# A graph network on one core: first part rearranged, with idle-time products, widened products and held-back loads

## The chip, the cores and the metric

The kernel runs on one core of one Trainium2 chip. The metric is the time of one execution on the device in microseconds, as the median of the runs shown; lower is better. Engines: PE (TensorE, matrix products), DVE (VectorE), ACT (ScalarE), POOL (GpSimd), SP (SyncE, which here only starts DMA transfers).

## The reference

Sixteen graphs of 512 nodes with 128 features, and a 512x512 adjacency matrix each. Four layers follow one another, each added to its input and normalised over the features:

```python
x = _layernorm(x + _L0_gnn_ref(x, adj, ...))   # adj @ (x @ weight) + bias
x = _layernorm(x + _L1_gnn_ref(x, adj, ...))   # five groups among 25 nodes, two layers each
x = _layernorm(x + _L2_gnn_ref(x, adj, ...))   # exp(e_n + f_m) * adj, rows normalised, times h
x = _layernorm(x + _L3_gnn_ref(x, adj, ...))   # 17-tap convolution, exp(-distance) * adj, gated update
```

`_L1` touches only the first 25 nodes of each graph. For each of five groups of them it forms `dinv * (A + 1) * dinv` from the group's rows and columns, multiplies by x and W1 (128x256), applies a relu, and does the same again with W2 (256x128). The fused sum is weighted by a softmax of `fusion_w`.

## The kernel before

The program is written out by hand: for each engine one list of instructions, with a semaphore wait wherever an instruction needs another engine's result. Nothing is reordered, so a wait holds up all that stands behind it on its engine. It has two parts with a barrier between them.

The **first part** (lines 318 to 1022) does graph 0 up to its third layer, the grouped layer of all other graphs, and the preparation of the weights.

- Graph 0: `adj_nat[0]` is transposed (L902, sixteen 128x128 products with the identity). ACT and DVE split the result into two rounded halves, `aT_hi` and `aT_lo` (L465, L531), so that `three` (L247 to L249) can multiply at reduced precision in three products of 512 columns. `AG_BANK` receives the aggregation, L921 multiplies by `w0`, and DVE adds the input (L628, `dv_y1`). Then come statistics, the inverse root on POOL (L391, `pow`) and the normalised `x1`. The second aggregation, of exp-weighted rows (`x_hi`, `x_lo` from L491 and L722), runs through the same `three` and signals `pe_agg2`; L979 and L772 make `y3`.
- Grouped layer of graph 0: masked blocks `A5[:, 0]` (L613) from `A0`, a copy of the first 25 rows and columns; degrees, their power on POOL (L387), scaled and transposed blocks (L623, L826, L633), then `U0` (L928), hidden layer (L942, ten products of 25 columns with `hw1`), `S0` (L952 with `hw2`) and the mix (L958).
- Grouped layer of graphs 1 to 15: they lie in three tiles of five graphs (`PT`, `PJ`), 125 rows each. `A0` holds their five 25x25 blocks on the diagonal of a 125x125 block, zero elsewhere, loaded by DMA into a zeroed tile (L369, L325, L327). `transpose_rows(t)` (L819) transposes the first 25 rows of each adjacency matrix, loaded as `adjP` (L330). `own_sums(t, graphs)` (L841) multiplies, for each graph, four chunks of x (`xt[t]`, stationary, 128 columns) by the graph's own 25 columns of `aPT`. `own_outputs` (L848) multiplies by `w0`; DVE adds and normalises (`x1P`, L750 to L781). L1003 and L1004 form U for all groups. Then, for each of five groups, `hidden` (L861), `second_layer` (L870) and `mix_nodes` (L879) alternate on PE with ACT (`relu_hidden`, `copy_s2`) and DVE (`add_group`).
- Weights: `transpose_weights(k)` (L884), four 128x128 blocks at a time, `round_weights` on ACT and `rest_of_weights` on DVE. `W_BANK` and `LATE` say which PSUM bank a block uses and behind which group it is done.
- Graph 1: its adjacency matrix is transposed (`transpose_second`, L891) and split.

SP starts the loads in the order of lines 321 to 362 (about 14 MB by the end of the first part); ACT starts the loads of small vectors.

The **second part** (from L1024) is a loop over the graphs in which the fourth layer of one graph is interleaved with the first three of the next. Its first PE instruction is L1485. `distances` (L1453) multiplies 13 rows of `LR`, two halves of 512 columns written by ACT, into 128x512 distances, four times for each graph. `msg_bias` and `ones_r` have 64 rows.

## Time and profile before

| | us |
|---|---|
| three runs | 646.16, 649.4, 648.75 |
| their median | 648.75 |
| the profiled execution | 646.53 |
| its span, first to last instruction | 644.7 |
| mean granted clock of PE | 0.961 |

| engine | busy us | share of span |
|---|---|---|
| PE, products | 605.6 | 94% |
| PE, weight loads (beside the products) | 494.5 | 77% |
| DVE | 491.4 | 76% |
| ACT | 314.0 | 49% |
| POOL | 111.8 | 17% |

The page comes from one profiled execution. A share is an average over both parts. The granted clock has two levels, 1.2 and 2.4 GHz, shown as 0.50 and 1.00; a number between them is a mean over a slice in which it changed. A product of two f32 operands appears as two records of PE, a transpose and a product of rounded operands as one. The end of a record is modelled and overlaps the next one, so the pace of several is read from their starts or from a merged row.

### The profile page before, as it was taken

What the parts mean: (1) busy time and instruction counts of PE and PEld (TensorE: products, weight loads), DVE (VectorE), ACT (ScalarE), POOL (GpSimd) and SP (SyncE); (2) the same over time, 40 slices, a digit from 0 to 9 for tenths busy, and PEclk for the clock granted to TensorE, in tenths of its full rate; (3) what the DMA queues carried; (4) which work ended last, traced back from release to release, by engine and by line L of the source; (5) the groups of instructions that cost most, each with busy time, mean ns of one, the idle gap of its engine ahead of it and who ended that gap; (6) DMA issues with size and microseconds to landing.
All of it is one profiled execution on the core that took longest, in us unless ns stands there. A gap on an engine that the chain in (4) does not pass through costs nothing.

```text
span 644.7 us, 11585 instructions
## 1 busy us (share of the span) xinstructions
PE 605.6 (94%) x3553; PEld 494.5 (77%) x3553; DVE 491.4 (76%) x1833; ACT 314.0 (49%) x635; POOL 111.8 (17%) x118
## 2 busy tenths in 40 slices
PE   3799798999999999999999999999999999999893
PEld 2689686878797879797878787878787887879672
DVE  4547653878888888878888889797979797978753
ACT  2201363464646465556464645555464646464331
POOL 2410101121121212030212120212121212112100
PEclk9757898999999999999999999999999999999998
DMA  7880002200303030303030303030201102000000
GB/s 193 244 262 2 1 1 89 91 1 1 100 2 98 0 98 0 98 0 98 0 98 0 98 0 98 0 96 2 70 28 40 58 22 78 6 13 1 18 17 16
DMA packets 33522, 34.50 MB, mean 54 GB/s; under 512 B 1882, under 2 KB 22753, under 8 KB 33368
## 3 DMA queue, kind: packets, MB, share of 16 engines
q1 hardware_dynamic: 33154, 34.03, 17.1%
q8 instruction: 13, 0.21, 0.1%
q10 hardware_dynamic: 342, 0.15, 0.1%
q14 instruction: 13, 0.11, 0.0%
HBM read 29.79 MB, written 4.39 MB: 53 GB/s over the span
## 4 chain that ended last, share of the span: by engine, by line
PE 44%; issue 22%; DVE 11%; POOL 3%; ACT 3%; DVEq 0%; POOLq 0%; ACTq 0%
PE bank L247 6%; PE bank L249 5%; PE bank L248 5%; PE pair L247 4%; PE pair L249 4%; PE pair L248 4%; PE bank L1582 4%; POOL rs L1085 3%; PE pair L1518 3%; DVE x L1236 2%; DVE st L1219 2%; PE bank L1453 2%; PE bank L1485 2%; PE bank L1523 1%; DVE mv L1225 1%
## 5 line engine op out<-in xcount | busy, mean ns | idle before, releaser
L1085 POOL TENSOR_TENSOR rs<-ve,neg_half 128x4 f32<-128x4 f32 (+1 forms) x61 | 58.1, 952 | 332.4 <-DVE ve L1231 299.6
L247 PE MATMUL bank<-cd_hi,w_hi 128*128 128x256 f32 x272 | 81.3, 299 | 0.0
L249 PE MATMUL bank<-cd_hi,w_lo 128*128 128x256 f32 x272 | 76.8, 282 | 0.0
L248 PE MATMUL bank<-cd_lo,w_hi 128*128 128x256 f32 x272 | 76.7, 282 | 0.0
L247 PEld LDWEIGHTS bank<-cd_hi,w_hi 128*128 128x128 f32 x272 | 51.6, 190 | 11.8 <-issue 11.7
L1582 PE MATMUL bank<-P,msg 128*128 128x512 f32 x128 | 57.6, 593 | 0.2 <-issue 0.2
L247 PE MATMUL pair<-aT_hi,x_hi 128*128 128x512 f32 x128 | 52.3, 409 | 0.0
L248 PE MATMUL pair<-aT_lo,x_hi 128*128 128x512 f32 x128 | 51.6, 403 | 0.0
L248 PEld LDWEIGHTS bank<-cd_lo,w_hi 128*128 128x128 f32 x272 | 51.5, 189 | 0.0
L249 PE MATMUL pair<-aT_hi,x_lo 128*128 128x512 f32 x128 | 51.5, 402 | 0.0
L249 PEld LDWEIGHTS bank<-cd_hi,w_lo 128*128 128x128 f32 x272 | 51.3, 189 | 0.0
L1263 DVE TENSOR_TENSOR P<-bank,aT 128x512 f32<-128x512 f32 x64 | 41.0, 681 | 3.9 <-ACT bank L1126 3.9
L1250 DVE TENSOR_TENSOR aT_lo<-bank,aT_hi 128x512 fp32r<-128x512 f32 x56 | 37.3, 686 | 7.9 <-ACT aT L1122 7.9
L247 PE MATMUL bank<-co_hi,w_hi 128*128 128x256 f32 x144 | 41.7, 289 | 0.0
L1582 PEld LDWEIGHTS bank<-P,msg 128*128 128x128 f32 x128 | 23.1, 190 | 23.3 <-issue 23.3
L249 PE MATMUL bank<-co_hi,w_lo 128*128 128x256 f32 x144 | 40.2, 280 | 0.0
L248 PE MATMUL bank<-co_lo,w_hi 128*128 128x256 f32 x144 | 40.2, 279 | 0.0
L1095 POOL TENSOR_TENSOR x<-x_nat,bias 128x512 f32<-128x512 f32 x15 | 19.5, 1303 | 90.9 <-DVE x3T_lo L1277 90.9
L1126 ACT ACTIVATE bank<-bank 128x512 f32<-128x512 f32 x64 | 34.4, 575 | 1.9 <-PE bank L1453 1.9
L1442 PEld LDWEIGHTS bank<-ident,adj_nat 128*128 128x128 f32 x224 | 25.9, 141 | 12.2 <-issue 7.4
L1122 ACT ACTIVATE aT<-bank 128x512 f32<-128x512 f32 x56 | 34.3, 613 | 0.0
L1267 DVE CUSTOM_DVE_ANT_0 prod<-x,v 128x128 f32<-128x128 f32 x120 | 29.0, 288 | 6.3 <-DVE x L1344 3.2
(326 smaller groups left out, 1543.0 us busy)
## 6 DMA issues: line engine op xcount, KB each, us to landing
adj_nat<-in_adj_dram SPq DMA_DIRECT2D x16, 1024.0 KB, 5.8
x_nat<-in_x_dram SPq DMA_DIRECT2D x16, 256.0 KB, 3.0
out_dram<-y_out SPq DMA_DIRECT2D x16, 256.0 KB, 2.4
xt<-in_x_dram SPq DMA_DIRECT2D x3, 1280.0 KB, 10.3
hw<-in_L_gnn_W_dram SPq DMA_DIRECT2D x2, 640.0 KB, 14.2
xt<-in_L_gnn_conv_w_dram SPq DMA_DIRECT2D x1, 1088.0 KB, 6.9
aT<-in_adj_dram SPq DMA_DIRECT2D x5, 150.0 KB
nat_ih<-in_L_gnn_w_ih_dram SPq DMA_DIRECT2D x1, 384.0 KB, 5.2
```

The costliest lines, as they stand in the source:

```text
L247: nc.tensor.matmul(o, lh, rh, start=start, stop=False)
L248: nc.tensor.matmul(o, lh, rl, start=False, stop=False)
L249: return nc.tensor.matmul(o, ll, rh, start=False, stop=stop)
L1085: g.tensor_tensor(rs[i][:, 0:n], ve[i][:, 0:n], neg_half[:, 0:n], ALU.pow).then_inc(po_rs[i], 1)
L1095: g.tensor_tensor(x1[:, :, :], x_nat[1 - par][:, :, :], bc(bias0[:, :], NC), ALU.add).then_inc(po_xb, 1)
L1122: s.activation(aT[par][:, mc, :], AT_BANK[mc % 2][:, :], ACT.Identity).then_inc(ac_aT[mc], 1)
L1126: s.activation(AT_BANK[mc % 2][:, :], AT_BANK[mc % 2][:, :], ACT.Exp, scale=2.0).then_inc(ac_E[mc], 1)
L1250: v.tensor_tensor(aT_lo[:, mc, :], AT_BANK[mc % 2][:, :], f(aT_hi[:, mc, :]), ALU.subtract).then_inc(dv_aTlo[mc], 1)
L1263: v.tensor_tensor(P[:, mc, :], AT_BANK[mc % 2][:, :], aT[par][:, mc, :], ALU.mult).then_inc(dv_P[mc], 1)
L1267: return v.tensor_tensor_reduce(prod[:, j, c, :], x2[:, c, :], v12[:, j, :], 1.0, 0.0, ALU.mult, ALU.add, ef[:, j, c:c + 1])
L1442: last = t_.transpose(AT_BANK[mc % 2][:, ch(c)], adj_nat[par][:, c, ch(mc)], ident[:, :])
L1582: last = t_.matmul(X_BANK[:, :], msg[:, ch(mc)], P[:, mc, :], start=(mc == 0), stop=(mc == NC - 1))
```

## The change

- Loads: the DMA copies of the diagonal blocks are gone. DVE builds `AB`, 25 columns to a tile, from `adj_nat[0]` and `adjP` and a folded identity `EY`, and the mask products read it five times over; the block-diagonal mask `BD` is made on POOL by two selects and multiplied into `GM`. SP waits for `adj_in[0]` before the first x tile and for `q_adjP` before W1; W2 and the fusion bias come behind the smaller weights.
- PE: 32 transposes of the identity are put between the mask transposes and the wait for the adjacency matrix. The first aggregation moves ahead of `transpose_rows`. The products of 25 columns (`own_sums`, the hidden layer of graph 0, the transposes of its blocks) take 100 columns, 75 of them the neighbours', and ACT copies out the 25 that count.
- Order: on all engines the work is sorted anew. `own_sums(2)`, `own_outputs` and the first weights come ahead of the second aggregation. The normalisation of the grouped rows comes ahead of graph 0's third sum, and the first groups ahead of most of graph 1's transposes and of the convolution weights (`LATE`, `LATE_AT`). The sums of taps (`nat_sum`) move from DVE to POOL.
- Second part: `LR` is filled with zeros once by POOL, and `distances` reads 128 rows. `msg_bias` and `ones_r` have 128 rows, the new ones of `msg_bias` zero.

The diff, cut to its core:

```diff
-        LATE = [[4], [5], [6, 7], [8], []]
+        LATE = [[], [2, 3], [4, 5], [6, 7], [8]]
+        LATE_AT = [[2], [3], [], [], []]
...
-                sp.wait_ge(q_zero, 1)
                 rows = a["adj"][1:B].rearrange("(t j) n m -> j n t m", j=PJ)
-                sp.dma_start(A0[0:NODES, 0, 0:NODES], a["adj"][0, 0:NODES, 0:NODES]).then_inc(q_blk, 16)
-                for j in range(PJ):
-                    sp.dma_start(A0[NODES * j:NODES * (j + 1), 1:NT, NODES * j:NODES * (j + 1)],
-                                 rows[j, 0:NODES, :, 0:NODES]).then_inc(q_blk, 16)
                 for j in range(PJ):
                     sp.dma_start(adjP[NODES * j:NODES * (j + 1), :, :], rows[j, 0:NODES]).then_inc(q_adjP, 16)
...
+                sp.wait_ge(adj_in[0], 16)
                 x_tile(0)
-                sp.dma_start(hw1[:, :, :], a["L1_gnn_W1"].rearrange("g i h -> i g h")).then_inc(q_h, 16)
-                sp.dma_start(hw2[:, :, :, :], a["L1_gnn_W2"].rearrange("g (h p) o -> p g h o", h=2)).then_inc(q_h, 16)
                 for dst, src in ((fw[:, 0, :], a["L1_gnn_fusion_w"].partition_broadcast(128)),
-                                 (hb2[:, :, :], a["L1_gnn_b2"].partition_broadcast(128)),
                                  (ab_col[:, :], a["L2_gnn_a_b"].partition_broadcast(128))):
                     sp.dma_start(dst, src).then_inc(q_cst2, 16)
-                sp.dma_start(nat_ww[:, 0, :], a["L2_gnn_W_w"]).then_inc(q_ww, 16)
-                sp.dma_start(nat_ww[:, 1, :], a["L3_gnn_w_msg"]).then_inc(q_ww, 16)
+                sp.wait_ge(q_adjP, 16 * PJ)
+                sp.dma_start(hw1[:, :, :], a["L1_gnn_W1"].rearrange("g i h -> i g h")).then_inc(q_h1, 16)
+                sp.wait_ge(q_zero, 1)
+                sp.dma_start(nat_ww[:, 0, 0:D], a["L2_gnn_W_w"]).then_inc(q_ww, 16)
+                sp.dma_start(nat_ww[:, 1, 0:D], a["L3_gnn_w_msg"]).then_inc(q_ww, 16)
                 sp.dma_start(nat_se[0:3, :], a["L3_gnn_w_se"]).then_inc(q_ww, 16)
+                sp.dma_start(hb2[:, :, :], a["L1_gnn_b2"].partition_broadcast(128)).then_inc(q_cst2, 16)
+                sp.dma_start(hw2[:, :, :, :], a["L1_gnn_W2"].rearrange("g (h p) o -> p g h o", h=2)).then_inc(q_h2, 16)
...
+                pool.wait_ge(q_sc2, 1)
+                pool.wait_ge(q_TT, 2)
+                g.tensor_tensor(nat_sum, nat_c2[:, :, 0:TAPS - 1:2], nat_c2[:, :, 1:TAPS:2], ALU.add).then_inc(q_sum, 1)
...
+                copy_sums(1)
+                round_weights(-1)
+                copy_sums(2)
                 act.wait_ge(dv_f, 1)
                 s.activation(pef[:, 1, :], ef[:, 1, :], ACT.Exp, bias=c12[:, 1:2]).then_inc(ac_pf, 1)
                 hold(act, ac_pf, 1)
                 for c in range(NC):
                     s.activation(x_hi[:, c, 1:D], x2[:, c, 1:D], ACT.Identity, scale=pef[:, 1, c:c + 1]).then_inc(ac_xs[c], 1)
-                copy_sums(1)
-                round_weights(-1)
+                round_weights(0)
...
+                def mask_blocks(t):
+                    for gi in range(NG):
+                        last = v.tensor_tensor_reduce(A5[0:R, t, gi, :].rearrange("p (j n) -> p j n", j=PJ),
+                                                      bc(AB[0:R, t, :], PJ),
+                                                      GM[0:R, gi, :].rearrange("p (j n) -> p j n", j=PJ), 1.0, 0.0,
+                                                      ALU.mult, ALU.add, deg[0:R, 3, NG * t + gi:NG * t + gi + 1])
+                    return last
...
+                for i in range(32):
+                    t_.transpose(bank[7][:, 0:D], ident[:, :], ident[:, :])
...
-                pe.wait_ge(q_adjP, 16 * PJ)
-                transpose_rows(0)
-                transpose_rows(1)
+                pe.wait_ge(q_gm, 2)
...
-                            last = t_.matmul(TT_BANK[t][:, NODES * j:NODES * (j + 1)], xt[t][:, j, mc, :],
-                                             aPT[t % 2][:, mc, NODES * j:NODES * (j + 1)], start=(mc == 0), stop=(mc == NC - 1))
+                            lo = 0 if j < PJ - 1 else NODES
+                            last = t_.matmul(TT_BANK[t][:, 100 * j:100 * (j + 1)], xt[t][:, j, mc, :],
+                                             aPT[t % 2][:, mc, lo:lo + 100], start=(mc == 0), stop=(mc == NC - 1))
...
+                for i in range(2 * NG):
+                    last = t_.matmul(bank[2][:, NODES * i:NODES * (i + 4)], hw1[:, i // 2, ch(i % 2)],
+                                     U0[:, i // 2:i // 2 + 4, :].rearrange("p g n -> p (g n)"), start=True, stop=True)
+                last.then_inc(q_hid0, 1)
...
+                own_sums(1, (0,))
...
+                block_rows(1)
+                block_rows(2)
+                block_rows(3)
+                own_sums(1, range(1, PJ))
+                pe.wait_ge(q_nT, 2)
+                own_sums(2, range(PJ))
                 pe.wait_ge(q_own, 5)
                 pe.wait_ge(q_sc1, 1)
                 transpose_weights(-1)
-                pe.wait_ge(q_nT, 2)
-                own_sums(2, (0, 1, 2))
+                pe.wait_ge(q_TTs, 2)
+                for t in range(PT):
+                    last = own_outputs(t)
+                last.then_inc(q_o, 1)
+                pe.wait_ge(q_whi, 1)
+                pe.wait_ge(q_wt, 16 * 3)
+                pe.wait_ge(q_sc1, 2)
+                transpose_weights(0)
...
+            g.memset(f(LR[:, :, :]), 0.0).then_inc(po_LR0, 1)
...
-                    t_.matmul(AT_BANK[mc % 2][:, :], LR[0:KD, 0, ch(mc)], LR[0:KD, 1, :], start=True, stop=True
+                    t_.matmul(AT_BANK[mc % 2][:, :], LR[:, 0, ch(mc)], LR[:, 1, :], start=True, stop=True
```

The order in which the engines now work is told by the program's own list. Three places of it follow. First PE at the start, before (the three products of `three` stand once of four times in each list):

```order
L897 MATMUL pair<-ident,adj_nat 125x125 x5
L902 MATMUL bank<-ident,adj_nat 128x128 x16
L819 MATMUL bank<-ident,aT 128x125 x8
L247 MATMUL pair<-aT_hi,x_hi 128x512
L248 MATMUL pair<-aT_lo,x_hi 128x512
L249 MATMUL pair<-aT_hi,x_lo 128x512
L917 MATMUL bank<-ident,vrows 128x27
L921 MATMUL pair<-w,agg_sb 128x128 x4
L826 MATMUL pair<-ident,A 25x25 x5
L841 MATMUL bank<-aPT,xt 128x25 x12
```

and in the change:

```order
L921 MATMUL pair<-ident,adj_nat 125x125 x5
L924 MATMUL bank<-ident 128x128 x32
L928 MATMUL bank<-ident,adj_nat 128x128 x16
L249 MATMUL pair<-aT_hi,x_hi 128x512
L250 MATMUL pair<-aT_lo,x_hi 128x512
L251 MATMUL pair<-aT_hi,x_lo 128x512
L842 MATMUL bank<-ident,aT 128x125 x8
L944 MATMUL pair<-w,agg_sb 128x128 x4
L849 MATMUL pair<-ident,A 25x100 x5
L865 MATMUL bank<-aPT,xt 128x100 x4
```

The idle-time products (L924) stand ahead of the adjacency transposes, and the aggregation has changed places with the eight transposes of node rows. The products of 25 columns have 100.

Second, PE ahead of the second aggregation and behind it (L979 before and L1021 now is the product with the attention weights, L1003 before and L1029 now the grouped products; rows that repeat a pattern are left out), before:

```order
L884 MATMUL bank<-ident,nat_w 128x128
L884 MATMUL bank<-ident,nat_ww 128x128
L884 MATMUL bank<-ident,nat_se 128x128
L841 MATMUL bank<-aPT,xt 128x25 x12
L247 MATMUL pair<-aT_hi,x_hi 128x512
L841 MATMUL bank<-aPT,xt 128x25 x4
L979 MATMUL pair<-plainT,agg_sb 128x130 x4
L841 MATMUL bank<-aPT,xt 128x25 x4
L848 MATMUL bank<-w,TTs 125x128 x3
L891 MATMUL bank<-ident,adj_nat 128x128 x4
L884 MATMUL pair<-ident,nat_hh 128x128 x3
L1003 MATMUL bank<-nadjT,x1P 128x125
```

and in the change:

```order
L865 MATMUL bank<-aPT,xt 128x100 x36
L908 MATMUL bank<-ident,nat_w 128x128
L908 MATMUL bank<-ident,nat_se 128x128
L872 MATMUL bank<-w,TTs 125x128 x3
L908 MATMUL bank<-ident,nat_c 128x128
L908 MATMUL bank<-ident,nat_ih 128x128 x2
L249 MATMUL pair<-aT_hi,x_hi 128x512
L915 MATMUL bank<-ident,adj_nat 128x128 x4
L1021 MATMUL pair<-plainT,agg_sb 128x130 x4
L908 MATMUL bank<-ident,nat_ih 128x128 x4
L1029 MATMUL bank<-nadjT,x1P 128x125
```

All products with the x tiles and the products with `w0` (L872) now stand ahead of the aggregation, and only four adjacency transposes, the attention product and four weight blocks between it and the grouped products.

Third, the loads on SP, before:

```order
L321 DMA x_nat<-in_x_dram 128x4x128
L322 DMA adj_nat<-in_adj_dram 128x4x512
L325 DMA adj_nat<-in_adj_dram 25x25
L327 DMA adj_nat<-in_adj_dram 25x3x25 x5
L330 DMA aT<-in_adj_dram 25x3x512 x5
L333 DMA xt<-in_x_dram 128x5x512
L336 DMA hw<-in_L_gnn_W_dram 128x5x256
L337 DMA hw<-in_L_gnn_W_dram 128x10x128
L341 DMA fw<-in_L_gnn_fusion_w_dram 128x5
L341 DMA hb<-in_L_gnn_b_dram 128x640
L341 DMA ab_col<-in_L_gnn_a_b_dram 128x1
L342 DMA nat_ww<-in_L_gnn_W_w_dram 128x128
```

and in the change:

```order
L324 DMA x_nat<-in_x_dram 128x4x128
L325 DMA adj_nat<-in_adj_dram 128x4x512
L328 DMA aT<-in_adj_dram 25x3x512 x5
L331 DMA xt<-in_x_dram 128x5x512
L337 DMA fw<-in_L_gnn_fusion_w_dram 128x5
L337 DMA ab_col<-in_L_gnn_a_b_dram 128x1
L339 DMA hw<-in_L_gnn_W_dram 128x5x256
L341 DMA nat_ww<-in_L_gnn_W_w_dram 128x128
L342 DMA nat_ww<-in_L_gnn_w_msg_dram 128x128
L343 DMA nat_se<-in_L_gnn_w_se_dram 3x128
L344 DMA hb<-in_L_gnn_b_dram 128x640
L345 DMA hw<-in_L_gnn_W_dram 128x10x128
```

The diagonal blocks are gone, and W2 (the second `hw` row) comes behind the smaller weights. The x tile waits for the landing of the adjacency matrix, the first `hw` row for that of the node rows.

## Rows read from the trace of the kernel before

**Rows 1.** The page: the span, PE's share, and the granted clock in 40 slices.
```profile
span 644.7 us, 11585 instructions
...
PE 605.6 (94%) x3553; PEld 494.5 (77%) x3553; DVE 491.4 (76%) x1833; ACT 314.0 (49%) x635; POOL 111.8 (17%) x118
...
PEclk9757898999999999999999999999999999999998
```
**Rows 2.** Stretches: busy us (count) of PE, PEld, DVE, ACT, POOL; granted clock, DMA share, GB/s.
```profile
13.90:17.30 3.40, 0.00 (x0) 0.00 (x0) 3.02 (x21) 0.33 (x1) 0.47 (x1) 1.00 1.06 207
17.30:24.10 6.80, 4.74 (x15) 4.08 (x16) 3.43 (x31) 1.18 (x2) 3.68 (x1) 0.50 0.73 208
...
31.00:48.00 17.00, 15.75 (x71) 14.52 (x72) 8.84 (x30) 1.40 (x5) 4.33 (x3) 0.50 0.83 267
...
54.90:65.10 10.20, 10.20 (x42) 9.43 (x42) 6.91 (x28) 2.36 (x9) 0.56 (x1) 0.50 0.00 1
...
75.30:82.20 6.90, 5.62 (x17) 4.17 (x18) 6.21 (x16) 2.66 (x6) 1.01 (x1) 0.51 0.00 0
82.20:102.60 20.40, 17.24 (x139) 16.00 (x137) 10.96 (x19) 10.90 (x25) 0.00 (x0) 1.00 0.00 1
102.60:106.10 3.50, 2.82 (x9) 2.46 (x10) 0.58 (x1) 1.08 (x2) 0.00 (x0) 0.51 0.18 52
106.10:604.00 497.90, 496.28 (x2933) 400.46 (x2933) 412.34 (x1565) 270.27 (x542) 92.35 (x89) 1.00 0.14 45
```
**Rows 3.** PE in order of time: start us, us, what [idle before].
```profile
9.92 3.67 PE L902 MATMUL bank<-ident,adj_nat 128*128 128x128 f32 x16 [6.37 <-DMA adj_nat<-in_adj_dram]
19.36 1.95 PE L819 MATMUL bank<-ident,aT 125*128 125x125 f32 x8 [5.77 <-DMA aT<-in_adj_dram]
...
44.91 3.90 PE L952 MATMUL pair<-hw,hT 128*25 128x128 f32 x20
...
50.84 5.05 PE L841 MATMUL bank<-aPT,xt 128*128 128x25 f32 x40
...
69.68 0.82 PE L884 MATMUL bank<-ident,nat_ih 128*128 128x128 f32 x6
...
88.22 1.48 PE L870 MATMUL bank<-hw,aPT 128*125 128x128 f32 x12
```
**Rows 4.** PE in order of time, at the marks and around them.
```profile
56.40 5.16 PE L841 MATMUL bank<-aPT,xt 128*128 128x25 f32 x24
...
65.72 0.40 PE L249 MATMUL pair<-aT_hi,x_lo 128*128 128x512 f32 x1
...
74.05 0.52 PE L884 MATMUL pair<-ident,nat_hh 128*128 128x128 f32 x3 [3.12 <-DVE y L772]
...
77.69 0.76 PE L1003 MATMUL bank<-nadjT,x1P 125*128 125x125 f32 x2 [0.29 <-issue]
...
91.43 1.48 PE L870 MATMUL bank<-hw,aPT 128*125 128x128 f32 x12
...
103.28 1.09 PE L1485 MATMUL bank<-ident,x 128*128 128x128 f32 x4 [2.59 <-PEq L1027]
```
**Rows 5.** DVE in order of time, the first sum and the scaling of columns.
```profile
27.35 0.69 DVE L628 TENSOR_TENSOR x<-pair,x 128x512 f32<-128x512 f32 x1 [5.42 <-PE pair L921]
...
33.99 2.25 DVE L650 TENSOR_TENSOR A<-A,deg 125x625 f32<-125x625 f32 x3
```
**Rows 6.** GpSimd in order of time, two powers.
```profile
16.82 4.16 POOL L387 TENSOR_TENSOR deg<-deg,neg_half 25x5 f32<-25x5 f32 x1 [7.35 <-DVE deg L538]
29.90 1.05 POOL L391 TENSOR_TENSOR rs<-ve,neg_half 128x4 f32<-128x4 f32 x1 [8.92 <-DVE ve L583]
```
**Rows 7.** Line L1453, the distance products: duration ns min/median/max.
```profile
L1453 PE MATMUL bank<-LR x64: 382/442/497, 118.6 to 622.2; 13*128 13x512 f32 x64
```
**Rows 8.** DMA issues to 130 us: KB each, median us to landing.
```profile
xt<-in_x_dram SPq DMA_DIRECT2D x3, 1280.0 KB, 10.3
hw<-in_L_gnn_W_dram SPq DMA_DIRECT2D x2, 640.0 KB, 14.2
```

335 lines of the change are left out of this document (170 added, 165 removed).

## The prediction

> **What bounds the kernel now.** The page comes first: TensorE (PE) is busy 94% of the 644.7 us span, and the granted clock is below full in the first sixth of the slices and at the very end [rows 1]. The table of stretches then splits the kernel in two. From 106.1 to 604.0 us PE is busy 496.28 of 497.90 us at clock 1.00: the loop over the graphs is bound by PE, and the change alters only its distance products. The first part (graph 0 and the grouped rows of the others) ends at about 103 us and has no single bound. The clock stood at half speed from 17.3 to 24.1, 31.0 to 48.0, 54.9 to 65.1 and 75.3 to 82.2 us, with PE busy 36.3 of these 40.9 us [rows 2]. So the view to read there is PE in order of time, against the clock.
>
> It shows two losses [rows 3]. One is idle PE: 6.37 us until the adjacency matrix lands at 9.92, then 5.77 us until the node rows land at 19.36, with the first aggregation queued behind them. The other is work at half clock: the clock falls at 54.9 while PE is fully occupied with 25-column products (L841 from 50.84), and had come back at 48.0 during the 128-column products of L952. An occupied PE need not hold the clock up. A 25-column product is bound by loading its weights: 40 records in 5.05 us at full clock (0.126 us each, two to a product), as much as a record of the 128-column L870, 12 in 1.48.
>
> **The change, part by part.** I follow the kernel to four marks of before: the first residual sum (DVE L628, 27.35 us [rows 5]), the end of the second aggregation (66.1), the products of the grouped rows (L1003, 77.69) and the first product of the second part (L1485, 103.28) [rows 4]. Hand-overs between engines count 0.1 to 0.3 us each, an estimate from the gaps in the rows. Full clock is assumed first.
>
> *To the first sum.* The 32 idle-time products start behind the mask transposes, at 3.5 us. They take 0.23 us each at the speed of L902 (16 in 3.67) and 0.11 once the clock is up (L884, 6 in 0.82 less the tail of the last) [rows 3], and fit before 9.9. Then the 16 adjacency transposes take 1.8 us, not 3.67. DVE takes the four chunks at L628's 0.69 for 512 columns [rows 5], from 11.2 to 13.9. The first aggregation, no longer behind the node rows, ends at 14.7, its output product at 17.2. DVE has graph 0's masked blocks and degrees at 15.2. Then GpSimd's power, 4.16 us in L387 [rows 6], ends the stage at 19.4, for the DVE step that waits for it stands ahead of the sum. The sum starts at 19.8: **-7.5 us**. New mask work on DVE and GpSimd, 1 to 2 us by L628's rate, lies before 8 us, where both wait for loads.
>
> *To the end of the second aggregation.* PE from 19.8: five graphs of four products at 0.25 (5.0), transposes and columns 1.2, ten hidden products (2.5), two attention products 0.6, the ten of L952 (2.5 at full clock), hand-overs 0.8: 32.4. Widening 25 columns to 100 costs nothing, for the weight load covers it: L870 has 128 columns in the same time. If nothing covered it, 75 more columns would be at most 75/128 of L870's 0.123 us a record, 0.14 a product, 10 us for the 70 widened ones; I take the row nearest in kind, L870, which is already as wide. Next DVE is late: two passes over 640 columns, eight small steps and the column scalings, 2.25 in L650 [rows 5], end at 35.9; PE's block transposes at 36.5. Nine graphs remain, 9.0 us, to 45.6. Weight transposes, ACT's copies (now ahead of the exponential on its queue) and the first scaled rows lead to 48.0, and twelve 512-column products of 0.23 end at 50.9. The stage takes 31.1 us against 38.7: **-7.6 us**.
>
> *To the grouped products.* Before, PE waited 3.12 us for graph 0's third sum (L772) [rows 4] and transposed weights ahead of them. Now DVE does their normalisation first: some 3,000 columns from 48.9 at L628's rate, 4.1 us, and nine hand-overs, to 54.2. The stage takes 3.3 us against 11.6: **-8.3 us**.
>
> *To the second part.* The five groups took 3.2 us each (L870 at 88.22 and 91.43) [rows 3, 4]. What was moved behind now lies in them: two adjacency transposes, two more weight blocks, the rests of x and of the bias on DVE. That gives PE 3.0 to 4.3 us in a group and DVE 3.9 in the third. Chained by hand, the first group starts at 59.3 and the second part at 80.3. The stage takes 26.1 us against 25.6: **+0.5 us**.
>
> *Around it.* The 64 distance products go from 13 rows to 128, at a median of 442 ns now [rows 7]; L249 in the last row before 66.1 has 128 rows, 512 columns and 0.40 us [rows 4]: nothing. The zero fill of LR and the sum of taps move to or lie on GpSimd, 1 to 3 us each by L391's kind of speed, 1.05 us [rows 6]; the one has 15 us until ACT writes LR, the other 8 us until its transpose. If their cover were gone they would cost that much.
>
> The sum is -7.5 - 7.6 - 8.3 + 0.5 = **-22.9 us** at full clock.
>
> *The clock's part.* PE still idles from 17.2 to 19.8 and in pieces between 51 and 60. No fall at all is the lower bound. I take two stretches like the shortest one seen, 3.5 us from 102.6 to 106.1 [rows 2]; each costs half its length, +3.4 together. The upper bound is rival 1. That gives -19.5 on the profiled execution's own 646.53, so 627.0; the runs' median, 648.75, is 2.2 higher. I put the median at **628**.
>
> *A rule against the change.* Before its fall at 17.3 the table has the clock at 1.00, and the only products since 3.6 us are the 16 adjacency transposes, at the 0.23 us of half clock [rows 2, 3]. A fall needs a clock that was up, so I read that transposes raise it (the page prints 1.00 from the start, which their durations contradict). The Trainium skill, "TensorE: Matmul & The Clock Gate", Part 4 on PE-mode transpose, says that full clock does not engage for transpose mode. By that rule the idle-time products are useless, which is rival 3.
>
> **Loads.** SP now holds the first x tile until the matrix has landed, and W1 until the node rows have; everything behind on its queue waits along, so the order in which loads are needed decides. Rival 2 prices that.
>
> **The rivals.**
> 1. *The widened products do not hold the clock.* For it: L841 did not hold it. Against: L870 with 128 columns ran from 85 to 99 at full clock [rows 2, 3]. The 60 products of the x tiles then take 0.43 us (24 records in 5.16 [rows 4]), 0.18 more each, 10.8 in all; with 2 for the work between them and less the 3.4 counted, +9: 637.
> 2. *Loads come late.* W2, the second and the third x tile are used at 29.8, 32.4 and 40.5; from issue to landing took 14.2 us for a weight and 10.3 for a tile [rows 8]. For: behind two waits W2 goes out at about 20 and with the old delay lands at 34, 4 late, its tile another 2. Against: less is in flight around it. 634.
> 3. *Transposes leave the clock down.* 32 x 0.23 = 7.4 us from 3.5 end at 10.9, a microsecond behind the matrix, and the 16 transposes keep their 3.67. The stage ends 2.9 later: 631.
> 4. *Slower: full rows cost in the loop.* If a distance product doubles with its rows filled, 64 x 0.44 = +28 us on PE, the bound there: 656. It decides from 0.31 us more a product. Against: L249, as above.
> 5. *The moves bring nothing.* DVE, or the order of the moved work, takes back what idle PE gives, in the second and the last stage: only the first stage's gain stays, 640. Against: DVE is busy 8.84 of 17.0 us from 31 to 48 [rows 2].
>
> **Chances.** Forecast 0.60, by itself 620 to 633 (the low end with no fall of the clock and a first power of 1.05 us, which DVE's masks then replace as the end of the stage); rival 1 0.17, rival 2 0.10, rival 3 0.07, rival 5 0.04, rival 4 0.02. Range 619 to 638. Half a per cent, 3 us, is about what a measurement tells from no change. Faster 0.96, same 0.02, slower 0.02: all but rival 4 and a rest lie over 3 us below.
>
> **What would show it.** The first sum near 20 us, the second aggregation ending at 51 to 54, the grouped products at 54 to 58, the second part at 80 to 86; the 100-column products at 0.126 us a record and clock 1.00; distances at 0.44. I am wrong if PE waits for W2 or an x tile after 28 us, if the clock is half over the 100-column products, or if the loop's time per graph moves.

## The result, and the profile after

| | before | changed |
|---|---|---|
| runs, us | 646.16, 649.4, 648.75, 647.48 | 612.51, 617.41, 619.04, 611.69 |
| median | 648.12 | 614.96 |
| profiled execution, own time | 646.53 | 612.51 |
| its span, mean granted clock | 644.7, 0.961 | 610.4, 0.986 |

The ratio is 0.9494, with an interval of 0.9421 to 0.9567: 33 us faster. The sign was right; the forecast of 628.0 was 13 us too high, and 614.96 lies below the range's low end of 619.

The page of the changed kernel, the rows that answer to [rows 1]:

```profile
span 610.4 us, 11668 instructions
...
PE 582.8 (95%) x3587; PEld 490.6 (80%) x3587; DVE 490.5 (80%) x1836; ACT 313.7 (51%) x638; POOL 112.2 (18%) x123
...
PEclk9899989999999999999999999999999999999996
```

The table of stretches, answering to [rows 2] (busy us (count) of PE, PEld, DVE, ACT, POOL; granted clock, DMA share, GB/s):

```profile
3.37:6.65 3.28, 3.28 (x17) 3.28 (x17) 1.78 (x7) 0.00 (x0) 1.05 (x6) 1.00 0.74 235
6.65:14.20 7.55, 6.91 (x46) 5.62 (x44) 4.30 (x19) 3.98 (x6) 1.27 (x1) 1.00 0.78 207
14.20:16.90 2.70, 0.01 (x1) 0.00 (x0) 0.04 (x2) 0.60 (x1) 1.16 (x1) 0.99 1.02 226
16.90:20.30 3.40, 3.40 (x16) 3.36 (x16) 1.70 (x13) 1.66 (x3) 0.00 (x0) 0.51 0.73 233
20.30:78.30 58.00, 52.50 (x412) 47.59 (x410) 47.46 (x163) 23.94 (x62) 9.87 (x8) 1.00 0.40 125
78.30:81.70 3.40, 3.27 (x10) 2.79 (x11) 0.69 (x1) 1.08 (x2) 1.12 (x2) 0.50 0.21 56
81.70:600.00 518.30, 511.11 (x3083) 426.06 (x3082) 428.44 (x1607) 282.42 (x564) 94.30 (x91) 1.00 0.14 44
```

The clock is at half speed for 6.8 us in two stretches, where it was for 44.4 by [rows 2]. It falls at 16.90, behind PE's idle 2.70 us, and at 78.3, where the second part begins. The 1.00 of the first line does not fit the durations: at full speed 32 transposes would take some 3.5 us, and they took 5.23.

PE in order of time (start us, us, what [idle before]), answering to [rows 3, 4]:

```profile
3.37 5.23 PE L924 MATMUL bank<-ident 128*128 128x128 f32 x32
9.04 1.97 PE L928 MATMUL bank<-ident,adj_nat 128*128 128x128 f32 x16 [0.44 <-DMA adj_nat<-in_adj_dram]
...
16.90 1.94 PE L842 MATMUL bank<-ident,aT 125*128 125x125 f32 x8 [2.70 <-DMA aT<-in_adj_dram]
18.64 1.82 PE L944 MATMUL pair<-w,agg_sb 128*128 128x128 f32 x8
...
37.27 8.18 PE L865 MATMUL bank<-aPT,xt 128*128 128x100 f32 x72
...
50.34 0.39 PE L251 MATMUL pair<-aT_hi,x_lo 128*128 128x512 f32 x1
...
53.52 0.46 PE L1029 MATMUL bank<-nadjT,x1P 125*128 125x125 f32 x2 [0.50 <-issue]
...
56.63 1.53 PE L885 MATMUL bank<-A,hw 128*128 128x375 f32 x4 [0.62 <-ACT A L443]
...
78.42 1.08 PE L1521 MATMUL bank<-ident,x 128*128 128x128 f32 x4 [2.66 <-PEq L1060]
```

DVE's first sum, answering to [rows 5]:

```profile
20.50 0.69 DVE L656 TENSOR_TENSOR x<-pair,x 128x512 f32<-128x512 f32 x1 [1.73 <-PE pair L944]
```

GpSimd's first power, answering to [rows 6]:

```profile
14.22 1.16 POOL L394 TENSOR_TENSOR deg<-deg,neg_half 25x5 f32<-25x5 f32 x1 [5.58 <-DVE deg L550]
```

Against the forecast's marks of 19.8, 50.9, 54.2 and 80.3 us at full clock the profile has 20.50, 50.7 (50.34 and the last product), 53.52 and 78.42. The first part became 24.9 us shorter (103.28 less 78.42).

The other 9.4 us are not in the forecast at all: from the first product of the second part to the end of the span it was 541.4 us (644.7 less 103.3) and is 532.0. The turn of the loop, one graph, is shorter. The weight loads of its first line, four in each of 16 turns, run from 103.2 to 605.1 us before and from 78.4 to 570.6 now:

```profile
L1485 PEld LDWEIGHTS bank<-ident,x x64: 137/141/231, 103.2 to 605.1; 128*128 128x128 f32 x64
...
L1521 PEld LDWEIGHTS bank<-ident,x x64: 137/140/229, 78.4 to 570.6; 128*128 128x128 f32 x64
```

Over 15 turns that is 33.46 us a turn before and 32.81 now (three loads more than 15 turns, so both are 0.02 too large and their difference is right).

Around one pair of distance products the order of the loads shows what changed. PE and PEld in order of time, before:

```profile
320.10 0.28 PE L249 MATMUL bank<-cd_hi,w_lo 128*128 128x256 f32 x1
320.31 0.29 PEld L1453 LDWEIGHTS bank<-LR 13*128 13x128 f32 x2
320.31 0.73 PE L1453 MATMUL bank<-LR 13*128 13x512 f32 x2
320.97 0.19 PEld L247 LDWEIGHTS bank<-cd_hi,w_hi 128*128 128x128 f32 x1 [0.37 <-issue]
320.97 0.39 PE L247 MATMUL bank<-cd_hi,w_hi 128*128 128x256 f32 x1
321.20 0.28 PE L248 MATMUL bank<-cd_lo,w_hi 128*128 128x256 f32 x1
```

And changed:

```profile
290.69 0.28 PE L251 MATMUL bank<-cd_hi,w_lo 128*128 128x256 f32 x1
290.69 0.31 PEld L1489 LDWEIGHTS bank<-LR 128*128 128x128 f32 x2
290.81 0.62 PE L1489 MATMUL bank<-LR 128*128 128x512 f32 x2
291.04 0.19 PEld L249 LDWEIGHTS bank<-cd_hi,w_hi 128*128 128x128 f32 x1
291.26 0.28 PE L249 MATMUL bank<-cd_hi,w_hi 128*128 128x256 f32 x1
291.38 0.28 PE L250 MATMUL bank<-cd_lo,w_hi 128*128 128x256 f32 x1
```

With 13 rows, the load of the distance weights begins only at 320.31, where the product before has run out (0.21 us after its start; such products follow each other every 0.12), and the next 128-row load begins with its own product at 320.97. From 320.10 to 320.97 are 0.87 us. With 128 rows the load starts together with the product before (290.69) and the next one 0.22 us ahead of its product: from 290.69 to 291.26 are 0.57. So 0.30 us go up to the product behind the pair, and the product after that is late by 0.11 more (321.20 and 291.38): 0.41 in all. The second pair of a turn loses 0.29 up to the product behind it (325.72 to 326.70, now 296.08 to 296.77), the bias product with its 64 rows 0.28 (310.50 to 311.25, now 281.44 to 281.91).

A turn does not show all of this. Set side by side product by product, in eleven turns, PE of the kernel before falls behind by 0.36 us at the bias and by 0.40 at each pair of distances, 1.16 in all. It gets back 0.17 to 0.30 between the two pairs and 0.30 behind the second, where the products with `P` start, and 0.56 to 0.68 are left; the turn's 0.65 lies in that. Of the pairs' 0.80, then, some 0.5 is taken up, and of the bias's 0.36 nothing. That PE would have waited for its operands at these two places anyway is my reading and was not tested.

The view of the line before has the second pair's gap in all 15 turns:

```profile
L1453 PEld LDWEIGHTS bank<-LR x64: 181/183/185, 118.6 to 622.0; 13*128 13x128 f32 x64
...
  issue: 5.3, 15
```

and changed, where no idle time stands under it:

```profile
L1489 PE MATMUL bank<-LR x64: 387/390/397, 93.5 to 586.9; 128*128 128x512 f32 x64
```

### The profile page after: what moved, and what is told of

The parts are those of the page before. It is cut to its first block, busy times and chain, and to the rows that moved or that the text cites. A ratio compares the mean times of both kernels' runs of the same rounds, so it can differ in the third digit from the quotient of the medians.

```text
span 610.4 us, 11668 instructions
## 1 busy us (share of the span) xinstructions
PE 582.8 (95%) x3587; PEld 490.6 (80%) x3587; DVE 490.5 (80%) x1836; ACT 313.7 (51%) x638; POOL 112.2 (18%) x123
## 3 DMA queue, kind: packets, MB, share of 16 engines
q1 hardware_dynamic: 32724, 33.99, 17.7%
## 4 chain that ended last, share of the span: by engine, by line
PE 42%; issue 23%; DVE 15%; POOL 4%; ACT 3%; DVEq 1%; POOLq 0%; ACTq 0%
PE bank L249 5%; PE bank L251 5%; PE bank L250 5%; PE pair L249 5%; PE pair L250 4%; PE pair L251 4%; PE bank L1618 4%; POOL rs L1119 4%; PE pair L1554 2%; DVE st L1255 2%; DVE x L1272 2%; PE bank L1521 2%; DVE mv L1261 1%; ACT aT_hi L1154 1%; PE bank L1559 1%
## 5 line engine op out<-in xcount | busy, mean ns | idle before, releaser
L249 PE MATMUL bank<-cd_hi,w_hi 128*128 128x256 f32 x272 | 77.7, 286 | 0.0
L249 PEld LDWEIGHTS bank<-cd_hi,w_hi 128*128 128x128 f32 x272 | 51.5, 189 | 1.5
L249 PE MATMUL pair<-aT_hi,x_hi 128*128 128x512 f32 x128 | 52.1, 407 | 0.6 <-DVE x_lo L763 0.3
L251 PE MATMUL pair<-aT_hi,x_lo 128*128 128x512 f32 x128 | 50.7, 396 | 0.0
L249 PE MATMUL bank<-co_hi,w_hi 128*128 128x256 f32 x144 | 41.6, 289 | 0.0
L1154 ACT ACTIVATE aT_hi<-bank 128x512 fp32r<-128x512 f32 x56 | 33.7, 603 | 0.0
```

Source lines behind the costliest of these rows:

```text
L249: nc.tensor.matmul(o, lh, rh, start=start, stop=False)
L251: return nc.tensor.matmul(o, ll, rh, start=False, stop=stop)
L1154: s.activation(aT_hi[:, mc, :], AT_BANK[mc % 2][:, :], ACT.Identity)
```

## The experiments

All kernels are the changed one or the one before with the edit shown. A "turn" is the mean of 15 turns of the loop in the profiled execution, "start" the first product of the second part. Each was compared with runs of the kernel before on the same chip (medians 646.66 to 647.62). Runs of one kernel spread over up to 7 us, so a difference of 2 us between medians of four is weak. The turn is steadier: 32.80 to 32.82 in nine profiles with the loop of the changed kernel (32.74 and 33.10 in two others), 33.46 to 33.49 in four with the loop of the kernel before (33.57 in a fifth). The "start" is not steady, for it holds the landing of the first loads and the clock's fall behind them: profiles of the versions with wide products have 0 to 17 us at half clock there, of which up to half is lost.

### The rows in the loop

**The kernel before, with full rows alone.**

```diff
+            g.memset(f(LR[:, :, :]), 0.0).then_inc(po_LR0, 1)
-  LR[0:KD, 0, ch(mc)], LR[0:KD, 1, :]
+  LR[:, 0, ch(mc)], LR[:, 1, :]
```

(and `msg_bias`, `ones_r` with 128 rows.)

> The kernel before with the zero-filled rows alone (LR, msg_bias and ones_r at 128 rows). Theory A, a product of fewer than 128 rows stops PE from loading weights ahead, at its own load and at the next one: the second part still starts near 103.3 us, a turn of the loop takes 32.9 us instead of 33.5, the span is about 9 us shorter, 635. Theory B, the loop of the changed kernel is shorter because of the state in which the first part leaves it (order of loads, overlap of the first turns): a turn stays at 33.5 and the span at 645.

Measured: 638.64 (636.05 to 641.3), ratio 0.9862 (0.9831 to 0.9893); a turn took 32.85 us instead of 33.46. The loop gets its 9 us with nothing else changed. The second part was expected to start near 103.3 as before and started at 107.3 in the profiled execution, the longest of the four: up to there the clock was at half speed for 51.2 us instead of 40.9.

**The changed kernel with 13 rows, with a bias of 64 rows, with 32 rows, and with 13 and 64.**

```diff
-  LR[:, 0, ch(mc)], LR[:, 1, :]
+  LR[0:13, 0, ch(mc)], LR[0:13, 1, :]
...
-  ones_r[:, :], msg_bias[:, :, :]
+  ones_r[0:64, :], msg_bias[0:64, :, :]
```

> The changed kernel with the distance products at 13 rows again. Theory A: the weights of a distance product are loaded after the product before it has ended, and so are those of the product behind, as in the kernel before; a turn is 0.4 to 0.6 us longer than 32.9 (two places in it), 6 to 9 us over the run: 617 to 621. Theory B: a turn of 32.9 and a span of 610.

> The changed kernel with the two bias products at 64 rows again. Theory A: one place in each turn, 0.2 to 0.3 us a turn, 3 to 4 us over the run: about 614. Theory B: no difference, 610.

> The changed kernel with the distance products at 32 rows, 13 filled and 19 zero. Theory A in two forms: if only a full 128 rows let weights be loaded ahead, this is like 13 rows, a turn of 33.3 to 33.5 us; if an odd number of rows was the trouble and whole blocks of 32 suffice, a turn stays at 32.9.

> The changed kernel with both row counts of the loop put back: 13 rows in the distance products, 64 in the message bias. Theory A (each place with part of the rows costs its own stall; 13 rows alone gave 33.12 us a turn, 64 rows alone 33.19, the changed kernel 32.82): the costs add, a turn takes 33.46 to 33.5, as in the kernel before, the loop is 9.4 to 10.2 us longer, and the time is 622 to 626. Theory B (one stall hides the other): a turn takes 33.2, and the time is 618 to 621.

| | median | turn | start |
|---|---|---|---|
| changed | 614.96 | 32.81 | 78.4 |
| 13 rows | 618.84 | 33.11 | 78.8 |
| bias 64 rows | 618.24 | 33.19 | 84.6 |
| 32 rows (one run) | 617.88 | 33.11 | 79.8 |
| 13 and 64 | 625.35 | 33.47 | 82.0 |

The distances cost 0.30 us a turn, the bias 0.38, and they add up to the 0.66 of both; ratio of the last 0.9653 (0.961 to 0.9696). The signs were as expected and the sizes were not: 0.4 to 0.6 us had been expected of the distances and 0.2 to 0.3 of the bias. The 84.6 of the bias run is no effect of the bias: its profile has 13.6 us at half clock behind the node rows. 32 rows are no better than 13, and 64 cost the same kind of stall, so it is not the amount of rows that is paid for: among 13 and 32 (distances), 64 (bias) and 128 (both), only 128 let the loads run ahead. The view of the distance line with 32 rows:

```profile
L1489 PE MATMUL bank<-LR x64: 392/442/494, 95.0 to 593.3; 32*128 32x512 f32 x64
...
  issue: 5.3, 15
```

The idle 5.3 us are back to the digit. The Trainium skill, "TensorE: Matmul & The Clock Gate", Part 3, "The mechanism", says that PE pulls a weight load ahead of products in flight when it aims at a row group that does not conflict, or at the background buffer. The trace agrees for neighbours of 128 rows; a load of 13 rows among them, and the 128-row load behind it, were not pulled ahead here.

### The width of the products

**25 columns again** in `own_sums` and in graph 0's hidden layer.

```diff
-  TT_BANK[t][:, 100 * j:100 * (j + 1)], xt[t][:, j, mc, :], aPT[t % 2][:, mc, lo:lo + 100]
+  TT_BANK[t][:, o:o + NODES], xt[t][:, j, mc, :], aPT[t % 2][:, mc, NODES * j:NODES * (j + 1)]
```

> The changed kernel with 25 columns in place of 100 in the 240 products of the graphs' own columns and in the products of the first hidden layer. Theory A (wide products hold the clock: in the changed kernel it was full for own_sums; 72 of them took 8.18 us, 0.114 each, where 24 of 25 columns took 5.16 at a falling clock and 40 took 5.05 at full clock, 0.126 each): the clock falls to 0.50 at own_sums of tile 0 and stays there to the end of them at least, and the second part starts 4 to 12 us later than 78.4; the time is 619 to 627. Theory B (the width is no matter): the clock stays full over own_sums, a product takes 0.10 to 0.13 us as with 100 columns, the second part starts at 77 to 79.5, and the time is within 1 us of 614.96. The loop takes 32.8 us a turn by either.

Measured: 624.29 (622.7 to 627.97), ratio 0.9673 (0.9639 to 0.9707), start at 90.1. The stretches of this run:

```profile
16.70:23.50 6.80, 4.44 (x22) 4.18 (x23) 2.41 (x14) 1.66 (x3) 0.00 (x0) 0.51 0.73 204
23.50:26.90 3.40, 3.40 (x30) 3.09 (x28) 3.14 (x23) 1.43 (x4) 1.02 (x1) 0.98 0.97 231
26.90:40.60 13.70, 13.70 (x64) 12.69 (x64) 5.51 (x30) 1.80 (x7) 4.41 (x3) 0.51 1.05 341
40.60:50.80 10.20, 10.20 (x88) 9.48 (x86) 9.66 (x30) 1.08 (x4) 0.48 (x1) 0.99 0.39 138
50.80:61.00 10.20, 10.20 (x45) 9.70 (x45) 3.34 (x15) 2.73 (x10) 0.07 (x1) 0.50 0.00 1
```

and its own products with the x tiles:

```profile
45.76 10.91 PE L865 MATMUL bank<-aPT,xt 128*128 128x25 f32 x72
```

PE is busy all of the 10.20 us from 40.6 to 50.8 and the clock still falls at 50.8, among the narrow products. In the changed kernel 72 records of 100 columns take 8.18 us, 0.114 each, all at full clock. Four times the columns cost no time and hold the clock: 9.3 us, and the reading of [rows 3] by which an occupied PE need not hold it stands. It is not the chance of one profile: the mean granted clock was 0.958 to 0.970 in the four runs with 25 columns and 0.979 to 0.992 in ten of the changed kernel.

### Idle-time products

**The changed kernel without the 32 transposes, and the kernel before with them alone.**

```diff
-                for i in range(32):
-                    t_.transpose(bank[7][:, 0:D], ident[:, :], ident[:, :])
```

> The changed kernel without its 32 idle-time transposes; all else stays. Theory A (the transposes raise the granted clock: in the changed kernel it is full from 6.65 us on, and the first residual sum, DVE's addition with w0's product, starts at 20.50): without them the sixteen transposes of the adjacency matrix take about the 3.67 us that they took in the kernel before instead of 1.97, the 48 products of the first aggregation run at half clock for a part, and the sum starts later, at 21.5 to 25; the time is 1 to 5 us over the changed kernel's 614.96. Theory B (the rival after the skill's rule, transposes leave the clock down, and the clock rose for the adjacency matrix's work alone): nothing changes, the clock rises at the same place near 6.65, the sum starts at 20.5 and the time is within 1 us. Theory C: the products are late by 1 to 3 us, but the stage waits for the adjacency loads, which landed at 16.9, so the second part starts at 78 to 79 as before and the time is unchanged though the clock rises later.

> The kernel before with the 32 idle-time transposes alone, ahead of its transposes of the adjacency matrix. Theory A: the clock is full by 6 to 8 us, the sixteen transposes take about 2 us instead of 3.67, but the residual sum at 27.35 waited for a chain through the grouped layer's diagonal loads and power, not for PE's pace, so the time stays within 1.5 us of 646.5 (0.2%). Theory B (PE's pace set the first stage): the sum starts 2 to 4 us earlier, at 23.3 to 25.3, and the time is 642 to 645. Theory C (the clock of the first part has its fall at another place because it rose earlier): the first stage gains under 1 us, and the second part's start moves by up to 4 us either way from 103.3 with the stretches at half clock.

Measured: 614.65 (611.96 to 617.1), ratio 0.9517 (0.9493 to 0.9542), and 647.09, ratio 1.0011 (0.9986 to 1.0035). They raise the clock: without them the sixteen matrix transposes go at half speed. PE in order of time, without them:

```profile
9.01 3.67 PE L926 MATMUL bank<-ident,adj_nat 128*128 128x128 f32 x16 [5.44 <-DMA adj_nat<-in_adj_dram]
17.61 1.23 PE L842 MATMUL bank<-ident,aT 125*128 125x125 f32 x8 [1.50 <-DMA aT<-in_adj_dram]
```

But the 1.7 us that they save lie ahead of a wait for the node rows, and are worth nothing in either kernel. Of the first expectation theory C is what happened, of the second theory A. (In the first one's profile the clock did not fall until 78.8 us: PE came later to its wait for the node rows and idled only 1.50 us in it.) The Trainium skill, "TensorE: Matmul & The Clock Gate", Part 4 on PE-mode transpose, says that full clock does not engage for transpose mode. The trace says otherwise: nothing but transposes of the identity ran on PE from 3.37 to 8.6 us in the changed kernel, at 5.23 us for 32 where half speed takes 7.4, and the sixteen behind them took 1.97 and not 3.67.

**24 transposes in the wait for the node rows.**

```diff
                 last.then_inc(pe_agg1, 1)
+                for i in range(24):
+                    t_.transpose(bank[7][:, 0:D], ident[:, :], ident[:, :])
                 pe.wait_ge(q_adjP, 16 * PJ)
```

> The changed kernel with 24 more transposes of the identity (0.11 us each at full clock, 2.6 us) between the first aggregation, which ends at 14.2 us, and the wait for adjP, which landed at 16.9. Theory A (the half-clock stretch that begins at 16.9 comes of PE's idle 2.70 us before it): the clock stays full from 6.65 us on through own_sums, the stretches of 3.4 to 13.7 us at half clock that the profiles of this kernel and its variants show there are gone, and the median is 611 to 613.5. Theory B (the clock falls on the idle or sparse work elsewhere): a half-clock stretch stays, and the time is within 1 us of 614.96. Theory C (the products are in the way when adjP lands early): up to 1 us slower.

> The changed kernel itself once more, for a firmer comparison with the version that fills the wait (612.36 us, ratio 0.9453 with an interval of 0.9424 to 0.9481). Theory A (the half-clock stretch behind 16.9 us costs on average 2 to 3 us): 613.5 to 617, ratio 0.948 to 0.953, and profiles or runs with a mean granted clock of 0.98 are the long ones. Theory B (filling the wait is worth nothing): 611.5 to 613.

Measured: 612.36 (610.02 to 614.45, six runs), ratio 0.9453 (0.9424 to 0.9481); the changed kernel again 614.39 (611.02 to 618.38, six runs), ratio 0.9486 (0.9453 to 0.952). The stretches with the wait filled, then those of the changed kernel in its second profile:

```profile
14.20:18.50 4.30, 2.92 (x26) 2.59 (x24) 0.28 (x3) 0.60 (x1) 1.16 (x1) 1.00 0.87 172
18.50:80.10 61.60, 55.64 (x433) 50.58 (x434) 48.34 (x176) 25.96 (x66) 10.70 (x9) 1.00 0.42 130
```

```profile
14.00:18.60 4.60, 1.74 (x13) 1.40 (x12) 1.61 (x13) 1.21 (x3) 1.16 (x1) 0.99 0.81 175
18.60:28.80 10.20, 10.20 (x48) 9.21 (x48) 7.21 (x49) 2.60 (x6) 3.46 (x2) 0.50 0.95 292
28.80:83.50 54.70, 49.12 (x379) 44.32 (x379) 40.12 (x118) 22.88 (x60) 7.23 (x8) 1.00 0.28 89
```

With the wait filled the clock stays full to 80.1 us; in the changed kernel it falls behind the wait and stayed down 3.4 us in one profile and 10.2 in another. Much of its spread goes with that: over its runs the time follows the mean granted clock, from 611.02 us at 0.992 to 618.38 at 0.979, while the filled version stays at 0.988 to 0.995. What PE did in the wait decides in part only: behind an idle 1.41 us (here) and 1.50 (without the 32 transposes) the clock stayed full, behind 1.72 (the tile held longer, below) and all of 2.70 and more in versions of the changed kernel it fell. And the start, 78.9 here, is no earlier than the changed kernel's best, 78.4. The 2 us between the medians would be what the fall costs on average, but the intervals of the ratios overlap, so a lead is likely, not shown. It had the lowest median of all versions.

### Loads and order

**Loads not held, and the first x tile held longer.**

```diff
-                sp.wait_ge(adj_in[0], 16)
                 x_tile(0)
+                sp.dma_start(hw1[:, :, :], ...
+                sp.dma_start(hw2[:, :, :, :], ...
...
-                sp.wait_ge(q_adjP, 16 * PJ)
```

> The changed kernel with its first x tile, W1 and W2 started where the kernel before starts them, without SP's two added waits. Theory A (they take bandwidth from the adjacency matrices, whose landing at 16.9 us ends the first stage): adjP lands at 18 to 22, the first residual sum starts 1 to 5 us after its 20.50, and the second part starts as much later; the time is 616 to 620. Theory B (the gain of the first stage comes from the removed diagonal loads, not from holding): adjP lands at 16.5 to 17.5, and the time is within 1 us of 614.96.

```diff
                 sp.wait_ge(adj_in[0], 16)
+                sp.wait_ge(q_adjP, 16 * PJ)
                 x_tile(0)
```

> The changed kernel with its first x tile held until adjP has landed too. Theory A (bandwidth: adjP, whose landing at 16.9 us starts the next stage, shares it with the x tile): adjP lands 1 to 2 us earlier, but the x tile, issued at 15 to 16 us, lands at 19.5 to 21.5, where own_sums of tile 0 started at 21.36; the first residual sum starts at 18.5 to 19.5 and the time is 612.5 to 614.5. Theory B (the x tile is what comes late): PE waits for it 1 to 4 us before own_sums, and the time is 615 to 618.

Measured: 617.87 (616.46 to 618.24), ratio 0.9547 (0.9529 to 0.9565), node rows at 18.4; and 619.74 (615.69 to 621.25), ratio 0.9551 (0.9501 to 0.9601), node rows at 17.7 and PE idle for the tile. Holding is worth about 3 us by the medians of four runs, which is weak, and it is right as it stands: held longer, the tile is late. Both profiles also have the clock at half speed for longer than the changed kernel's 3.4 us, 13.6 and 17.1, so landing and clock are not told apart here.

```profile
23.98 2.00 PE L866 MATMUL bank<-aPT,xt 128*128 128x100 f32 x8 [1.89 <-DMA xt<-in_x_dram]
```

PE could begin with the adjacency matrix at 8.6 us in one of these profiles and only at 10.8 in another though nothing ahead of its load differed, and with the node rows at 16.9 to 20.4. So the landing of 17.7 says little against the 16.9; PE's wait for the tile says more.

**The node rows transposed first**, as in the kernel before.

```diff
                 pe.wait_ge(q_gm, 2)
+                pe.wait_ge(q_adjP, 16 * PJ)
+                transpose_rows(0)
+                transpose_rows(1)
                 pe.wait_ge(ac_xhi, 1)
```

> The changed kernel with the transposes of adjP's rows for tiles 0 and 1 put back ahead of graph 0's first aggregation, where the kernel before has them. Theory A (PE then stands still until adjP lands at 16.9 us, and the aggregation, 3 us from 11.21 to 14.2 in the changed kernel, runs behind it): the first residual sum starts at 23.5 to 26 instead of 20.50, the second aggregation ends 2 to 5 us later than 50.7, and the time is 617 to 620. Theory B (the gap is filled later, because own_sums waits for the x tile and not for PE): the sum is as late as A says, but the second part starts within 1 us of 78.4 and the time is within 1 us of 614.96.

Measured: 617.42 (615.92 to 620.05), ratio 0.9528 (0.9492 to 0.9563). In the profile PE idled 7.66 us for rows that landed late, at 20.36, and the sum started at 28.13, start at 86.0; of that lateness of 7.6 us some 3.5 belong to the landing. The median puts the order at 2.5 us, which from four runs is weak.

**Five parts undone together** (13 and 64 rows, 25 columns, no idle-time products, loads not held, node rows first).

> The changed kernel with five of its parts undone together: 13 and 64 rows in the loop, 25 columns, no idle-time products, loads not held, adjP's rows transposed ahead of the first aggregation. One by one these cost 10.4, 9.3, -0.3, 2.9 and 2.5 us over 614.96. Theory A (they add): 639 to 641, and the other 7 us to the kernel before (646.7) come from what is left, the diagonal blocks built on chip and the order of the first part behind the first aggregation. Theory B (they overlap, since late loads, a late aggregation and a clock that falls anyway cover one another): 632 to 637, and what is left is worth 10 to 15 us. Theory C (they aid each other): 643 to 648.

Measured: 638.43 (636.22 to 641.71), ratio 0.9847 (0.9813 to 0.9882), a turn 33.49, start 97.2. One by one the parts came to 10.4 + 9.3 - 0.3 + 2.9 + 2.5 = 24.8 us, together to 23.5: they add, within the spread. The remaining 8 us (646.7 less 638.4) are what was not taken apart, and nothing here shows which part of it earns them: the diagonal blocks built on chip instead of loaded, the new order behind the first aggregation, the sums of taps on GpSimd.

### The power of 4.16 us

The first power of degrees took 4.16 us in the profile of the kernel before and in both of its variants above, and 1.16 in the changed kernel, on the same 25x5 values. In the one it comes up 0.07 us behind the first of DVE's fifteen mask products (16.82 and 16.75), in the other beside an idle DVE.

```diff
+                pool.wait_ge(q_A1, 3)
                 degree_root(NODES, 0, NG, 1)
```

> The changed kernel in which GpSimd's first power waits until the diagonal blocks of tiles 1 to 3 are there, so that it runs beside DVE's five mask products of tile 1. Theory A (an elementwise GpSimd operation is slowed or blocked while DVE reads two operands of SBUF; 1.16 us in the changed kernel with DVE idle, 4.16 in the kernel before beside fifteen mask products): the power takes 1.9 to 3.5 us, or a mask product beside it takes 0.8 to 1.5 us in place of 0.28. Theory B (the 4.16 came from being the first power of the program): it takes 1.1 to 1.3 us again. The time is within 1.5 us of 614.96 by either, as the masked blocks of graph 0 are not waited for until 26.15.

```diff
+                pool.wait_ge(q_A1, 4)
                 degree_root(NODES, 0, NG, 1)
...
-                mask_blocks(1)
+                mask_blocks(1).then_inc(q_A1, 1)
+                mask_blocks(2)
```

> The changed kernel with GpSimd's first power started by the last of DVE's five mask products of tile 1 and the five of tile 2 put right behind these, so that the power comes up while DVE's stream of two-operand products is already running, as in the kernel before (16.82, behind the first of fifteen at 16.75; it took 4.16 us, to 20.98, where the stream ended at 20.1). In the last test the power came up 0.06 us ahead of the stream and took 1.16. Theory A (GpSimd waits until DVE's unbroken stream has ended): the power ends 0.8 to 1.2 us behind the stream's last product, and takes 1.9 to 2.4 us. Theory B (DVE's stream is no matter): 1.1 to 1.3 us.

> The changed kernel with GpSimd's first power started behind the five mask products of tile 1, as in the last test, where ten products over a 25-column operand that is read five times ran beside it and it took 1.16 us. Now ten products of the same size follow at once that read the identity, 125 contiguous columns, as the kernel before reads its diagonal blocks (their results are overwritten later). Theory A (it is the contiguous operand that holds GpSimd up): the power ends 0.7 to 1.2 us behind the stream's last product and takes 2.5 to 3.5 us. Theory B: 1.16 us again.

And in the kernel before, with the mask products put behind the power:

```diff
                 degrees(NODES, 0, NG, 1)
+                dve.wait_ge(q_dgp, 1)
                 for t in range(1, NT):
```

> The kernel before, in which DVE waits for GpSimd's first power before its fifteen mask products. Theory A (the fifteen products over contiguous operands hold GpSimd up): the power, 4.16 us in each profile of the kernel before, takes 1.1 to 1.3 us. Theory B (something else of that program or place): 4.16 us again, and DVE stands still for it. The time is 646 to 652 by either.

Measured for the power, in this order: 1.16, 1.16, 1.17 and 1.17 us. GpSimd in order of time in the last two:

```profile
20.34 1.17 POOL L394 TENSOR_TENSOR deg<-deg,neg_half 25x5 f32<-25x5 f32 x1 [11.62 <-DVE deg L563]
```

```profile
15.78 1.17 POOL L387 TENSOR_TENSOR deg<-deg,neg_half 25x5 f32<-25x5 f32 x1 [7.35 <-DVE deg L538]
```

Without the products beside it the power of the kernel before takes 1.17: it is not the first use that cost. But products beside it, of either layout and with the power started ahead of them or among them, did not slow it in the changed kernel. What it takes to hold the power up stays open; my theory of an unbroken or a contiguous stream fell. And it was worth nothing in the kernel before either: 646.97 us (one run), for DVE still ended its masks at 20.12 and the sum waited for PE. The times of the others are 615.61 (ratio 0.9506, 0.9463 to 0.9548), 618.4 and 619.2 (one run each); the last has a turn of 33.10 although its loop is the changed kernel's, which was not followed up.

## Why the prediction was right or wrong

The profiled executions differ by 34.0 us where the steps gave 19.5. The 14.5 missing are 9.4 in the loop, 3.4 for the clock and 1.9 in the marks (80.3 less 78.42): 14.7, the same within what lies around the spans. The measured marks hold what the clock did cost.

- **"Around it ... L249 ... has 128 rows, 512 columns and 0.40 us: nothing."** This is the step that failed, worth 9.4 us. The product itself does cost nothing more (390 ns against 442; the forecast had 0.44 us stay). The sign of being wrong that the forecast named, a loop whose time per graph moves, came true: 33.46 us to 32.81. I priced the product, and looked for what full rows might cost, but not for what partial rows already cost their neighbours: rival 4 had the opposite sign. The row was there to be read: under the line's durations the view of L1453 has 5.3 us of "issue" idle in 15 places, one a turn, in the one stretch that PE bounds, and a median (442) above that of a product with ten times the rows. The bias product, 64 to 128 rows, was not priced at all (the forecast has the change alter "only its distance products" in the loop) and was worth more, 0.38 us a turn against 0.30.
- **The first sum** (19.8, measured 20.50) came out near for a wrong reason. I let GpSimd's power of 4.16 us end the stage at 19.4. It took 1.16 and ended at 15.4; instead PE waited for the node rows to 16.90, with the output product queued behind their transposes, and both then ran at half clock. The low end of the forecast's own range took the short power and named the mask products as what would replace it; the node rows replaced it, which that text did not name: their landing has no term in the sum, though the output product stood behind them in the changed order. The nearness of 19.8 is luck.
- **The second aggregation** (50.9, 50.7) and **the grouped products** (54.2, 53.52) were right, by the steps as told. Widening was priced by L870 at nothing (0.114 us a record against 0.126); taking the width back confirms it.
- **The last stage** was put at 26.1 and took 24.9 (53.52 to 78.42): too dear by 1.2 us of the 1.9; the rest lies in the marks ahead. Its way to the first group was 2.0 us too dear (54.2 to 59.3, measured 53.52 to 56.63), the groups themselves 0.8 too cheap (21.0, measured 21.8).
- **The clock's part**, +3.4, was mis-sized. The profile has one stretch of 3.4 us inside the first part, not two, which costs 1.7 at most; it begins where PE's wait for loads ends. This term is also what varies from run to run: none, 3.4 and 10.2 us at half clock were all seen with at most idle-time products changed, and the median run is 2 us above the profiled one.
- **Rival 1** (the widened products do not hold the clock) did not occur: 25-column work does not hold it, the wide does, as the forecast weighed it. The price of narrow columns in the changed kernel is 9.3 us, near the 9 that it gave. **Rival 2** did not occur: W2 and the tiles were there in time (started early, W1, W2 and the tile made it 2.9 us slower). **Rival 3**, transposes leave the clock down, is refuted: they raise it. Its price of 2.9 us was wrong too, since the stage waited for the rows anyway. **Rivals 4 and 5** did not occur (rival 5's 640 should read 641, 648.75 less 7.5).

## What to carry to other kernels

Price an edit by what its instruction does to its neighbours as well: on a PE that bounds a loop, two products of fewer than 128 rows among full ones set PE back by 0.36 to 0.41 us at each place, and a turn of three places was 0.65 longer; zeros in the other rows cost nothing. Before costing a change at nothing, open the source view of the line it touches and account for every "issue" gap. Where a stage is bounded by narrow products, widening them under the cover of the weight load may pay by the clock alone, and where PE waits for a load, filling the wait may pay by the clock behind it, not by the work ahead of it.

## What was not expected of the hardware

- Rows: see above, 33.47 us a turn with 13 and 64 rows, 32.81 with 128.
- One operation of DVE took far longer beside one of GpSimd: DVE's product L611 took 1.09 us at 36.49 and 0.28 right after it, while GpSimd's addition L403 ran from 36.31 for 1.12 us. The Trainium skill, "SBUF — State Buffer", "SBUF: two separate sides", has the two engines lock a shared pair of ports for a whole instruction when DVE has two SBUF inputs and GpSimd reads SBUF; this row agrees. The power of 1.16 us beside products of two operands that went on at their usual pace, one every 0.21 us, does not.
- One kernel's first loads land at times 2 to 3 us apart from one execution to the next, and the time of one kernel spreads over 7 us, much of which goes with the clock's fall behind them.
